# The down product of an expert layer two steps behind its up product, on one core

## What is computed

```python
q, k, v = split(x @ Wqkv + bqkv)          # q and k centred along the columns
q2 = normalised(q * q); k2 = normalised(k * k)
kv = einsum('nc,nd->cd', k2, v)
x1 = layernorm(x + (v + q2 @ kv / sqrt(1024)) @ Wln + bln)
sel = sigmoid(x1 @ expert_sel.T)                       # 16 gates of a row
scores = relu(einsum('sd,edh->seh', x1, keys))         # up product, 16 experts, H = 128
out = layernorm(x1 + einsum('seh,ehv,se->sv', scores, values, sel))   # down product
```

## Time and profile before

| | |
|---|---|
| median of 3 runs | 1028.7 us (1028.34 to 1030.61) |
| the profiled execution | 1027.94 us |
| its span, first to last instruction | 1026.1 us |
| PE busy | 995.9 us, 97% |
| DVE busy | 815.5 us, 79% |
| ACT busy | 528.7 us, 52% |
| POOL busy | 213.9 us, 21% |
| mean granted clock of PE | 0.993 |

### The profile page before, as it was taken

How to read it: one execution, slowest core, us unless ns; L and a number is a source line. 1 busy time by engine, 2 the same in 40 slices (tenths; PEclk the granted TensorE clock), 3 DMA queues, 4 the chain that set the end, 5 groups by cost and what they waited for, 6 DMA issues and landing times.

```text
span 1026.1 us, 22008 instructions
## 1 busy us (share of the span) xinstructions
PE 995.9 (97%) x8324; PEld 979.6 (95%) x8324; DVE 815.5 (79%) x1874; ACT 528.7 (52%) x1150; POOL 213.9 (21%) x267
## 2 busy tenths in 40 slices
PE   7899999999999999999999999999999999999996
PEld 6799999999999999999999999999999999999996
DVE  5789887888868888688877889778887889867565
ACT  4566554465445654456544565356554466444332
POOL 0021212212221222212222112221221222122221
PEclk8999999999999999999999999999999999999999
DMA  5031111211122011220121210212111211110100
GB/s 183 22 121 66 44 63 42 86 62 43 63 84 83 21 44 66 80 101 25 32 77 61 103 43 31 75 63 85 43 63 42 85 63 43 63 43 33 33 22 21
DMA packets 47982, 62.20 MB, mean 61 GB/s; under 512 B 4098, under 2 KB 34562, under 8 KB 47876
## 3 DMA queue, kind: packets, MB, share of 16 engines
q1 hardware_dynamic: 47876, 60.79, 17.4%
HBM read 37.18 MB, written 23.07 MB: 59 GB/s over the span
## 4 chain that ended last, share of the span: by engine, by line
PE 77%; DVE 13%; ACT 5%; issue 4%; DMA 0%; DVEq 0%; POOL 0%; ACTq 0%; POOLq 0%
PE down_bank L1324 27%; PE up_bank L1324 27%; PE ring_bank L1324 8%; PE qk_bank L1324 7%; PE g_bank L1324 3%; DVE gated L1088 3%; DVE gated_l L1094 2%; ACT gated_h L553 2%; DVE qT_l L946 2%; ACT z L635 1%; DVE x1T_l L952 1%; PE ring_bank L1575 1%; PE ring_bank L1576 1%; PE g_bank L1370 1%; DVE z L990 1%
## 5 line engine op out<-in xcount | busy, mean ns | idle before, releaser
L539 POOL PARTITION_BROADCAST sel_all<-sel_rows x240 | 199.4, 831 | 680.3 <-DVE gated L1088 641.7
L553 ACT ACTIVATE gated_h<-gated 128x512 fp32r<-128x512 f32 x256 | 161.6, 631 | 303.2 <-DVE gated L1088 301.3
L1324 PE MATMUL down_bank<-vals_h,gated_h 128*128 128x256 f32 x1024 | 288.8, 282 | 5.8 <-DVE gated_l L1094 4.2
L1324 PE MATMUL up_bank<-x1T_h,keys_h 128*128 128x256 f32 x1024 | 285.4, 279 | 0.0
L1324 PE MATMUL up_bank<-x1T_l,keys_h 128*128 128x256 f32 x1024 | 285.3, 279 | 0.0
L1324 PE MATMUL up_bank<-x1T_h,keys_l 128*128 128x256 f32 x1024 | 285.3, 279 | 0.0
L1324 PE MATMUL down_bank<-vals_l,gated_h 128*128 128x256 f32 x1024 | 285.0, 278 | 0.0
L1324 PE MATMUL down_bank<-vals_h,gated_l 128*128 128x256 f32 x1024 | 285.0, 278 | 0.0
L1094 DVE TENSOR_TENSOR gated_l<-gated,gated_h 128x512 fp32r<-128x512 f32 x256 | 171.8, 671 | 51.6 <-ACT gated_h L553 49.9
L1088 DVE SCALAR_TENSOR_TENSOR gated<-up_bank,sel_all 128x512 f32<-128x512 f32 x256 | 176.1, 688 | 44.1 <-PE up_bank L1324 41.5
L1324 PEld LDWEIGHTS down_bank<-vals_h,gated_h 128*128 128x128 f32 x1024 | 192.6, 188 | 11.8 <-DVE gated_l L1094 6.7
(11 more groups left out here) (252 smaller groups left out, 1699.2 us busy)
## 6 DMA issues: line engine op xcount, KB each, us to landing
out<-z SPq DMA_DIRECT2D x32, 256.0 KB, 2.4
x_raw<-in_x SPq DMA_DIRECT2D x15, 512.0 KB, 4.8
xT_raw<-in_xT SPq DMA_DIRECT2D x14, 512.0 KB, 4.1
parked_q<-w_room SPq DMA_DIRECT2D x14, 512.0 KB, 3.0
q<-parked_q SPq DMA_DIRECT2D x56, 128.0 KB, 3.0
parked_x<-w_room SPq DMA_DIRECT2D x14, 512.0 KB, 2.6
z<-parked_x SPq DMA_DIRECT2D x56, 128.0 KB, 3.0
w_room<-in_keys SPq DMA_DIRECT2D x4, 512.0 KB, 3.4
```

The source lines that it names most:

```text
L539: nc.gpsimd.partition_broadcast(sel_all[:, e % 2], row, P).then_inc(sel_spread, 1)
L553: return nc.scalar.activation(dst, src, ACT.Copy, **kw)
L1324: last = mm(dst, lhs, rhs, start=start and i == 0, stop=stop and i == n - 1, **kw)
```

## The change

`LAG` goes from 1 to 2: a step's down product stands behind the up product two steps on, and gated_h, gated_l have three places (`HELD`). The place for that comes from `sel_rows`, which has three rooms in place of four (the last four rows of gates go to the first room in step 4, `move_last_rows`, and room j holds experts 4 j to 4 j + 3), and x1's turned tiles come back into `w_room` and no longer into `z`. DVE so waits, before the first tile of QS or XS goes to `w_room`, until XR has read it, and ZA no longer waits for that. The tables change: ZA from steps 1 and 17 to 2 and 18, ZN from 2, 3 and 19, 20 to 3, 4 and 26, 27; QS from 9 on to 11 on; QR 0 from 20 to 18, KV from 21 to 20, Y 0 to 3 (and XS 0 to 3 behind them) from 22 to 25 to 21 to 24, XR 0 from 29 to 28, bias_x 2 and 3 from 27, 28 to 30, 31. No matmul is added or removed.

```diff
-LAG = 1
+LAG = 2
+HELD = LAG + 1
...
-        1: [("ZA", 0), ("ZA", 1)], 2: [("ZN", 0), ("Y", 4)], 3: [("ZN", 1), ("XS", 4)], 4: [("Y", 5)],
+        1: [], 2: [("ZA", 0), ("ZA", 1), ("Y", 4)], 3: [("ZN", 0), ("XS", 4)], 4: [("ZN", 1), ("Y", 5)],
...
-        18: [("GG", 6), ("QS", 5)], 19: [("KS", 0), ("ZN", 0), ("GG", 7), ("QS", 6)],
-        20: [("QR", 0), ("ZN", 1), ("QS", 7)], 21: [("KV", 0)], 22: [("Y", 0)], 23: [("Y", 1), ("XS", 0)], 24: [("Y", 2), ("XS", 1)],
-        25: [("Y", 3), ("XS", 2)], 26: [("XS", 3)], 27: [("QR", 1)], 29: [("XR", 0)], 30: [("LG", 0)],
+        18: [("ZA", 0), ("ZA", 1), ("QR", 0), ("GG", 6)], 19: [("KS", 0), ("GG", 7), ("QS", 6)], 20: [("KV", 0), ("QS", 7)],
+        21: [("Y", 0)], 22: [("Y", 1), ("XS", 0)], 23: [("Y", 2), ("XS", 1)], 24: [("Y", 3), ("XS", 2)],
+        25: [("XS", 3)], 26: [("ZN", 0)], 27: [("QR", 1), ("ZN", 1)], 28: [("XR", 0)], 30: [("LG", 0)],
...
-        gated_h, gated_l = sb("gated_h", [P, 2, GN], F32R), sb("gated_l", [P, 2, GN], F32R)
+        gated_h, gated_l = sb("gated_h", [P, HELD, GN], F32R), sb("gated_l", [P, HELD, GN], F32R)
...
-        sel_rows = sb("sel_rows", [P, E // 4, GN])
+        sel_rows = sb("sel_rows", [P, ROW_ROOMS, GN])
...
-        turned_x = z[:].rearrange("p a t c -> p (a t c)")
+        turned_x = w_room[:]
...
-                else:
-                    for p in range(2):
-                        at_least(sp, stored[p], 16 * (2 * it + 1 - h))
...
+            def move_last_rows(grp):
+
+                sp.wait_ge(sel_spread, grp * E + 4)
+                j = ROW_ROOMS
+                sp.dma_start(sel_rows[0:P:32, 0], sel[4 * j:4 * j + 4, :]).then_inc(rows_in[j], 16)
...
-                    at_least(act, down_made, f - 1)
-                    copy(gated_h[:, s % 2], gated[:]).then_inc(gated_hi, 1)
+                    at_least(act, down_made, f + 1 - HELD)
+                    copy(gated_h[:, f % HELD], gated[:]).then_inc(gated_hi, 1)
...
-                    if 0 < it < B:
-                        dve.wait_ge(x1T_lo, tile(it, T - 1) if off == 0 else tile(it, GT - 1))
...
+                elif kind == "QS" and a < GT:
+                    dve.wait_ge(x1T_lo, tile(b - 1, T - 1))
+                elif kind == "XS" and a >= GT:
+                    dve.wait_ge(x1T_lo, tile(b, GT - 1))
...
                 early(it, s)
+                add_zs(it, s)
                 split_lo(it, s)
-                add_zs(it, s)
...
-                    r = (s - LAG) % 2
+                    r = f % HELD
```

More of the change, by code:

```diff
@@ L39 @@
     plan={
[1 row of a table removed]
[1 row of a table added]
         5: [("Y", 6), ("XS", 5)], 6: [("Y", 7), ("XS", 6)], 7: [("XS", 7), ("QK", 0)], 8: [("QK", 1)],
[7 rows of a table removed]
[6 rows of a table added]
     },
     split_xT={4: 0, 9: 1}, split_x={5: 0, 10: 1, 13: 2, 16: 3},
-    bias_x={9: 0, 14: 1, 27: 2, 28: 3},
+    bias_x={9: 0, 14: 1, 30: 2, 31: 3},
     gpsimd_xT=(), gpsimd_x=())
@@ L65 @@
 ROWS_STEP = 14
+ROW_ROOMS = 3
+LAST_ROWS_STEP = 4
 BLOCK = 32
@@ L195, in build_program @@
         k0_fourths = [pair_of(sel_rows[:, 1]), pair_of(sel_all[:, 1])]
-        k0_total, k0_fourth_total = pair_of(sel_rows[:, 2]), pair_of(sel_rows[:, 3])
+        k0_total, k0_fourth_total = pair_of(sel_rows[:, 2]), q2[:, 6:8]
         wvl_f, gT0 = pair_of(sel_all[:, 0]), pair_of(gated[:])
@@ L452, in move_rows @@
                 at_least(sp, sel_spread, (it + off) * STEPS + g * E)
-                for j in (1, 2, 3, 0):
-                    sp.dma_start(sel_rows[0:P:32, j], sel[j:E:4, :]).then_inc(rows_in[j], 16)
+                for j in range(ROW_ROOMS):
+                    sp.dma_start(sel_rows[0:P:32, j], sel[4 * j:4 * j + 4, :]).then_inc(rows_in[j], 16)
+            def move_last_rows(grp):
+                sp.wait_ge(sel_spread, grp * E + 4)
+                j = ROW_ROOMS
+                sp.dma_start(sel_rows[0:P:32, 0], sel[4 * j:4 * j + 4, :]).then_inc(rows_in[j], 16)
             def load_xT0(p):
@@ L496, in step @@
                     load_half(it, 0)
+                if s % E == LAST_ROWS_STEP and it < B:
+                    move_last_rows(G * it + s // E)
                 if s == 5 and has(it, 1):
@@ L528, in spread_group @@
                     at_least(pool, gate_applied, grp * E + (e - 1))
-                    i, j = divmod(e, 4)
+                    j, i = divmod(e, 4)
                     if e == 0:
@@ L534, in spread_group @@
                     else:
-                        if e <= 4:
+                        if i == 0 or e == 1:
                             at_least(pool, rows_in[j], grp * 16 + 16)
-                        row = sel_rows[32 * i:32 * i + 1, j]
+                        row = sel_rows[32 * i:32 * i + 1, j % ROW_ROOMS]
                     nc.gpsimd.partition_broadcast(sel_all[:, e % 2], row, P).then_inc(sel_spread, 1)
@@ L1093, in step @@
                     dve.wait_ge(gated_hi, f + 1)
-                    V.tensor_tensor(gated_l[:, s % 2], gated[:],
-                                    gated_h[:, s % 2].bitcast(F32), ALU.subtract).then_inc(gated_lo, 1)
+                    V.tensor_tensor(gated_l[:, f % HELD], gated[:],
+                                    gated_h[:, f % HELD].bitcast(F32), ALU.subtract).then_inc(gated_lo, 1)
                 if (it, s) == (0, 0):
@@ L1613, in step @@
                             at_least(pe, z_added, 2 * grp - 1 + a)
-                        if t == 2 and last_iteration(it):
+                        if t == 2 and last_iteration(it) and e == E - 1:
                             last.then_inc(last_half_made, 1)
```

## The result

| | before | changed |
|---|---|---|
| median of the runs on one chip | 1029.65 us (4 runs, 1028.34 to 1031.21) | 1017.13 us (4 runs, 1013.07 to 1022.25) |
| profiled execution | 1027.94 us | 1022.25 us |
| its span | 1026.1 us | 1020.5 us |

The ratio is 0.988 (95% interval 0.984 to 0.991): 1.2% less time, with an interval that lies clear of 1. The forecast was 1008.4 us, so the kernel gained less than forecast, and its executions differ by 9 us. Measured once more, as the first experiment, the median was 1022.56 and the ratio 0.992.

The account below looks back on a forecast made before the run. PE, busy 97%, was taken as the bound: its waits plus its fast or slow issue level. From the profiled 1027.94 us, -16.0 and -4.3 give 1007.6; the runs' median lies 0.8 higher, so 1008.4 us, range 998 to 1020.

Parts of the forecast that it names:

- the sum of the waits: PE's waits over the whole kernel: -14.2 + 0.5 - 2.3 = -16.0 us.
- the levels: PE's matmul starts, 0.113 or 0.118 us apart: fast share 68%, from 56%, giving -4.3 us (bounds +2 and -12).
- rival 2: Waits come back at LG and KV because DVE runs later than reckoned: 8.4 us more, 1016.8 us; chance 0.17.
- a fast share under 45%: Sign of being wrong: under 45% of PE's matmul distances at the fast level.
- count of fast distances near 5400: Sign of being right: about 5400 of PE's distances between matmul starts at the fast level, against 4401 before.
- (a): Down products waiting for gated_l, at steps 1, 3, 17, 26, 29 and the end: all waits go, -14.2 us.
- Margin 0.4: Step 18, ZA's sums before the down product: ready near 746.7, wanted at 747.1, so no wait but little room.
- (b): GG 2 in iteration 0, waiting for DVE: earlier savings return half as a longer wait, +0.5 us.
- (c): Logits at step 30: wait stays 0.6 us, no gain from moving XR 0; bounds 4.8 us gain or loss.
- (d): KV and Y: Y's 5.1 us wait for kvw_l ends, KV waits 0.4 us seven times, 2.8; net -2.3 us.
- Rival 1: Levels stay at 56% fast, so only the waits' -16.0 us counts: 1012.7 us; chance 0.2.
- rival 4: Slow level locked in after KS, nothing resetting PE, for all iterations: +3.8 us, 1032.5 us; chance 0.03.

Follow-up runs that it names:

- lag_alone: Kernel before with LAG = 2 but its old table (only ZA and ZN one or two steps later) and x1's turned tiles still in z: 1021.41 us, ratio 0.993.
- zn_early: Changed kernel with ZN 0 and 1 at steps 25 and 26 in place of 26 and 27: 1006.13 us, ratio 0.977.
- wide_21: Changed kernel with the up product of step 21 alone as 6 matmuls of 512 columns in place of 12 of 256: 1020.67 us, ratio 0.991.
- wide_all: Changed kernel with every up product as 6 matmuls of 512 columns in place of 12 of 256: 1017.11 us, ratio 0.988.

## Why the prediction was right and wrong

The sign was right, the sum of the waits nearly so, the levels wrong, and the total ended 8.7 us above the forecast. It stayed inside the stated range only by luck: the room up to 1020 was there for rival 2, waits that come back elsewhere, and what filled it was the levels, whose term had a bound of +2. By the ratio of the repeat, 0.992, the time would have been 1021.7, outside. Of the prediction's own signs of being wrong one was met in full, a fast share under 45%, and one in small, down products that come late at steps 2 and 18, where ZA stands. Of its signs of being right the count of fast distances near 5400 failed (2376 and 3282).

- **(a), right.** No down product of steps 1, 3, 17, 26 or 29 waits for gated_l in iterations 1 to 6, and the last three follow one another. Not foreseen: 0.26 us at step 2 in some iterations, where ZA now stands, and 0.38 once at step 18, 1.6 us of excess in all, iteration 7 included. "Margin 0.4" was thin where it was worked out, and step 2 wasn't worked out.
- **(b), the wrong place.** GG 2 of iteration 0 waits 0.84 us from start to start, less than the 1.11 of before, not more. A new wait stands ahead of it, 2.07 + 0.28 us for keys_l in step 4, which no step of mine had on its list; lag_alone has it too, so it comes with the lag.
- **(c), right, with its mechanism.** The logits wait 0.38 + 0.28 us: no gain from XR 0's move, because z's scalings stand ahead of it on ACT. Moving ZN removed the wait. What I did not see is that this wait, left in place, draws the level of up to 19 steps behind it.
- **(d), right in sign, smaller.** KV waits in 4 of 7 iterations, 0.2 us of excess on average for the 0.4 I took. Y waits nowhere.
- The waits together: -14.7 us for the -16.0 forecast. That is in part luck too: 2.3 us at keys_l and 1.6 us at steps 2 and 18, both unforeseen, are set off by 1.2 us less at KV, 0.8 less at GG 2 and 0.5 less at the logits.
- **The levels: the step that failed.** "I take 68% fast", -4.3 us; it was 30% and 41%, so +9.2 and +5.2 us, against a bound of +2. I had counted that KS left PE slow 5 times of 7 and that the Y wait left it fast 5 of 7, and then treated the removal of the Y wait as a pure gain of a wait. The list of what changes the level had no KV on it, and the draw after KV was reckoned as for any break. But KV left PE slow 14 times of 14 in the two executions of the change, and 7 of 7 already in the trace that the prediction was made from, twice coming from fast and without a wait. With the Y wait gone nothing stood between KV and the logits, and steps 20 to 30 went from 918 fast distances to 43 and 34, 3.9 and 4.0 us in iterations 1 to 6. lag_alone, where the Y wait stayed, kept fast stretches in 5 of 7 iterations. The rest is drawn: the other steps of iterations 1 to 6, behind the waits at the logits and at step 2, lost another 4.3 us in the profiled execution and nothing in the repeat.
- Rival 1, levels as before, would have been 1012.7, and rival 4, slow throughout, is where the profiled execution leans: its mechanism, that nothing resets PE once it is slow, is what happened for steps 20 to 30, with KV where it names KS. I gave it 0.03, since I asked for all iterations and all steps.
- The Trainium skill (TensorE: Matmul & The Clock Gate, Back-to-back issue gap) gives N / 2.4 + 2.5 ns at full clock, 109 ns for 256 columns, as the gap of an isolated matmul, which the prediction took without that limit; for a stream of weight loads and matmuls it gives about 131 ns for 512 columns, and no second level in either. By one gap, zn_early would gain the 3.0 us of waits over the changed kernel. Its profiled execution gained 16.3, of which 12.2 are the move from 30% to 64% at the fast level, and matmuls of 512 columns here follow one another at 226 to 236 ns. The measurement decides: the level is part of the sum.

Open stays what in PE sets the level. The runs show what left it how: KV slow 98 times of 98, KS slow whenever PE came to it fast, a wide up product fast at step 21 (35 of 35) and as it was at nearly every other step, unbroken logits fast at step 30 (28 of 28) but at step 11, of the times that PE came to them slow, in about a third, a wait one or the other. So it is not the kind of matmul alone, and the place counts. They don't show why.

## What to carry to other kernels

A wait is more than its length. Where an engine's pace depends on how its stream was last broken, ask of every wait that you remove which pace it left behind, and of every one that you leave whether it draws the pace of a long stretch: here waits of 3 us cost 11 to 16 together with what they drew. Ask the same of work that doesn't wait: KV turned PE slow without a break, and it could have been counted in the first trace. Before a product is made to lag, look in the side engines' streams for work that can stand elsewhere (z's scaling ahead of x1T_h on ACT): one line of the table gave about as much as the whole change. When you move such work, look at all its halves, on every engine (QR 0 left DVE's chain to k_l and entered ACT's). And a gain ahead of a wait for another engine is only moved there (lag_alone, wide_21) until that wait is gone.

## What was not expected of the hardware

- Matmuls of 128x128 by 128x256, back to back at full granted clock, follow one another at either 113.3 or 117.8 ns for hundreds of matmuls. The twelve of KV, at 118 to 120 ns, left PE at the slow level 98 times of 98, waiting or not. Eight matmuls of two columns (KS) turned it slow each of the 61 times that PE came to them fast. Six matmuls of 512 columns brought it back 35 of 35 times at step 21, four did 28 of 28 times at step 30, but 92 of 92 products of six elsewhere left it slow (wide_all).
- The first matmul after a wait is followed by the next 0.19 to 0.22 us later, not 0.11; of 512 columns 0.31. So a wait costs some 0.08 to 0.1 us more than the distance ahead of the first matmul shows.
- A matmul of 512 columns takes 0.226 to 0.236 us, no less than two of 256 at the fast level.
- The spread of a kernel's times differed by schedule: 9 us for the change, 1.3 us over four executions once the waits at steps 30 and 2 were gone, but 4.2 us with GG 7 first, where PE waits as little.
